# The opening of a two-layer adaLN kernel: raw weights in four homes over two queues, modulation in the filter's waits, the first normalisation between the spectra

## The reference, cut to what matters

```
h = layernorm(x) * (1 + ca) + sa ; x = x + ga * hyena(h)      # layer 0
h = layernorm(x) * (1 + cb) + sb ; x = x + gb * sign_ffn(h)
h = layernorm(x) * (1 + ca) + sa ; x = x + ga * attention(h)  # layer 1, 16 heads, causal
h = layernorm(x) * (1 + cb) + sb ; x = x + gb * experts(h)    # 2 of 8
gates: g = (2 * (g >= 0) - 1) * max(|g|, 0.25)
filter k = (sin-MLP of three layers on a position code) @ wo * decay
```

## Time and profile before

| | us |
|---|---|
| median of 3 runs (lowest, highest) | 1976.02 (1970.32, 1976.5) |
| the profiled execution | 1987.1 |
| its span | 1985.3 |
| first `up_rows` matmul in it | 115.12 |

### The profile page before, as it was taken

One profiled execution on the slowest core, in us unless ns is written; L12 is line 12 of the kernel. 1 busy time (PEld: TensorE's weight loads), 2 busy tenths in 40 slices (PEclk: granted clock), 3 DMA queues, 4 the chain that ended last, 5 costly groups with the idle time before them and its releaser, 6 DMA issues.

```text
span 1985.3 us, 27255 instructions
## 1 busy us (share of the span) xinstructions
PE 1790.3 (90%) x9220; PEld 1445.2 (73%) x9220; DVE 1455.8 (73%) x2643; ACT 997.5 (50%) x2142; POOL 684.9 (35%) x709
## 2 busy tenths in 40 slices
PE   6778879999988969999989979999999996999997
PEld 3657767777777857777877767777777785777786
DVE  4468877887468777887566887888746887888744
ACT  1132446777341437777632325677734143776742
POOL 0023244544123144553323234454412414455321
PEclk7879989999989979999989988999999997999999
DMA  6330054443060043443251024445225004354311
GB/s 241 110 129 1 9 157 112 98 123 76 28 259 1 1 127 102 124 109 80 50 217 54 0 57 125 107 99 132 60 71 211 1 1 127 102 131 125 77 28 48
DMA packets 90127, 184.14 MB, mean 93 GB/s; under 512 B 28991, under 2 KB 43135, under 8 KB 86790
## 3 DMA queue, kind: packets, MB, share of 16 engines
q1 hardware_dynamic: 82694, 168.77, 29.2%
q10 hardware_dynamic: 7296, 13.63, 2.4%
HBM read 125.46 MB, written 46.94 MB: 87 GB/s over the span
## 4 chain that ended last, share of the span: by engine, by line
PE 69%; DVE 12%; ACT 5%; issue 4%; DVEq 3%; POOL 3%; DMA 1%; ACTq 1%; SPq 1%; POOLq 0%; another core or an unknown queue 0%
PE ps L434 9%; PE ps L557 8%; PE ps L577 7%; PE ps L579 6%; PE ps L600 6%; PE ps L597 6%; PE ps L598 6%; PE ps L744 6%; PE ps L440 4%; PE ps L786 3%; PE ps L646 2%; PE ps L583 2%; PE ps L494 1%; PE ps L512 1%; ACT hT L823 1%
## 5 line engine op out<-in xcount | busy, mean ns | idle before, releaser
L1145 DVE CUSTOM_DVE_ANT_0 ps<-ps,mrow 128x128 f32<-128x128 f32 (+7 forms) x512 | 385.0, 765 | 118.2 <-PE ps L557 116.2
L1376 POOL TENSOR_TENSOR psplit<-pT,psplit 128x384 fp32r<-128x384 f32 (+3 forms) x320 | 302.3, 958 | 427.2 <-ACT psplit L866 425.1
L866 ACT ACTIVATE psplit<-ps 128x512 fp32r<-128x512 f32 (+3 forms) x768 | 373.2, 486 | 0.0
L865 ACT ACTIVATE pT<-ps 128x512 f32<-128x512 f32 (+3 forms) x512 | 256.7, 501 | 170.3 <-PE ps L583 91.0
L557 PE MATMUL ps<-khl,qhh 128*128 128x512 f32 (+3 forms) x768 | 252.9, 394 | 61.0 <-DMA qhh<-psplit 38.0
L577 PE MATMUL ps<-qhh,khl 128*128 128x512 f32 (+3 forms) x768 | 271.8, 354 | 7.6 <-ACT psplit L866 7.0
L579 PE MATMUL ps<-q,k 65*128 65x512 f32 (+3 forms) x768 | 268.5, 350 | 0.0
L597 PE MATMUL ps<-psplit,vhi 128*65 128x512 f32 (+3 forms) x768 | 264.8, 345 | 0.0
L600 PE MATMUL ps<-psplit,vhi 128*65 128x512 f32 (+3 forms) x768 | 259.8, 338 | 0.0
L598 PE MATMUL ps<-psplit,vlo 128*65 128x512 f32 (+3 forms) x768 | 259.3, 338 | 0.0
L557 PEld LDWEIGHTS ps<-khl,qhh 128*128 128x128 f32 x768 | 132.2, 202 | 80.1 <-issue 59.3
(11 more groups left out here) (188 smaller groups left out, 3402.8 us busy)
## 6 DMA issues: line engine op xcount, KB each, us to landing
qhh<-q_scratch SPq DMA_DIRECT2D x112, 256.0 KB, 5.1
q_scratch<-hrow SPq DMA_DIRECT2D x24, 1024.0 KB, 7.1
mix<-inverse_scratch SPq DMA_DIRECT2D x64, 256.0 KB, 3.5
q<-q_scratch SPq DMA_DIRECT2D x56, 256.0 KB, 4.6
Kf<-kf_scratch SPq DMA_DIRECT2D x3, 3072.0 KB, 20.5
khl<-k_scratch SPq DMA_DIRECT2D x24, 256.0 KB, 7.7
sgn<-sgn_scratch SPq DMA_DIRECT2D x6, 1024.0 KB, 14.1
x<-in_x SPq DMA_DIRECT2D x5, 1024.0 KB, 5.5
```

Of the source, the lines that this page charges most:

```text
L865: A(full(n)[:, 0:hi - lo], ps[:, b, 0:hi - lo], ACT.Exp, scale=SCALE)
L866: A(psplit[:, n % PRING, 0, 0:hi - lo], ps[:, b, 0:hi - lo], ACT.Exp, scale=SCALE)\
L1145: V.tensor_tensor_reduce(out=v, in0=v, in1=mrow[:, L - n:L], scale=1.0, scalar=-3e38, op0=ALU.add, op1=ALU.max, accum_out=mx[:, u % 2, i:i ...
L1376: G.tensor_tensor(psplit[:, n % PRING, 1, 0:m], full(n)[:, 0:m], psplit[:, n % PRING, 0, 0:m].bitcast(F32), ALU.subtract)\
```

## The change

- **Loads.** ScalarE issues five: cT, `wmod0`, `w2T`, `wmod1`, `in_w`. SyncE issues the rest. The four that filter layer 0 needs have a semaphore of their own; the other five have `loaded_layers`. `w1T`, the windows, `w1rows`, the two halves of `wqkv`, x and the (now 11) small ones have semaphores too.
- **Homes.** `wmod0` stays in `spare`, `wmod1` goes into `Kf` blocks 0 and 1, raw `in_w` into `Kf` block 3, the halves of `wqkv` into `wo` and `rope`, which are loaded after the split (`loaded_late`).
- **TensorE's order**: filter 0, three quarters of `modT` 0, filter 1, the last quarter, gate 0, `alpha2`, filter 2, `modT` 1, kernel rows, gate 1, spectrum 0, transposes of the first normalisation, spectra 1 to 3, then the batch. Setup banks are given by hand.
- **VectorE's order**: two angle steps, `modT` 0, third angle step, gate 0, `alpha1`, `modT` 1, kernel rows, gate 1, normalisation, split of `in_w`, `h_low`, mix 0, bounds of both gates, mix 1, split of `wqkv`, mix 2, split of `wr`, mix 3.
- **SyncE** asks for x as soon as the signs are taken, does not load it again for batch 0, and makes its stores after the `wqkv` split. The gate rows go after the three weight stores; VectorE waits for that store ahead of its spectrum products.
- **The meeting goes**, with the clearing. Counts run on from the setup: `at` adds `MADE`. One set of bank accounts serves both.

The core of the diff:

```diff
+SETUP = -1
+MADE = {"mod_picked": 1, "var_done": 2, "rstd_done": 2, "hrow_done": 8, "hT_done": 4, "h_lo_done": 4}
...
+            wmod = [wraw, Kf[:, 0:2, :, :].rearrange("p m k n -> p m (k n)")]
+            in_raw = Kf[:, 3, :, :].rearrange("p k n -> p (k n)").rearrange("p (q n) -> p q n", q=ND)
+            qkv_raw = [wo[:, :, :].rearrange("p q n -> p (q n)")[:, 0:QKV],
+                       rope[:, :, :].rearrange("p c n -> p (c n)")[:, 0:QKV]]
...
-        def part_ends(eng, name):
-
-            eng.drain().then_inc(bar, 1)
-            eng.wait_ge(go[name], 1)
-            eng.sem_clear(go[name])
...
# TensorE
+            filtered(0)
+            modulation(0, (0, 1, 2))
+            filtered(1)
+            modulation(0, (3,))
+            gate(0)
             pe.wait_ge(*at("const_made", 1))
             pe.wait_ge(*at("abs_done", 1))
-            b = bk.take(pe, ("alpha2",))
+            b = bk.take(pe, ("alpha2",), at=GATE_BANK[1])
             for q in range(NH1):
                 i = mm(ps[:, b, 0:D], ones[:, :], w2T[:, q, :], start=q == 0, stop=q == NH1 - 1)
             i.then_inc(ready[b], 1)
+            filtered(2)
+            modulation(1, (0, 1, 2, 3))
+            pe.wait_ge(*at("filter_sine", 3))
+            for t in range(0, NT, 2):
+                b = bk.take(pe, ("kern", t), until=at("kern_done", t // 2 + 1), at=(6, 7, 0, 1)[t // 2])
...
+            gate(1)
+            pe.wait_ge(*at("loaded_windows", 16 * 3))
+            pe.wait_ge(*at("kern_done", NT // 2))
+            kernel_spectrum(0)
...
             for h in range(NHALF):
                 normed(0, h)
-            part_ends(pe, "tensor")
+            for m in range(1, NB):
+                kernel_spectrum(m)
# ScalarE
+            load = nc.scalar.dma_start
+            load(cT[:, :, :, :], d["cT"], allow_slow_non_contiguous=True).then_inc(s["loaded_c"], 16)
+            load(wmod[0], d["wmod0"]).then_inc(s["loaded_mod0"], 16)
+            load(w2T[:, :, :], d["w2T"]).then_inc(s["loaded_w2"], 16)
+            load(wmod[1], d["wmod1"]).then_inc(s["loaded_mod1"], 16)
+            load(in_raw, d["in_w"]).then_inc(s["loaded_in"], 16)
...
+            sines(0)
+            act.wait_ge(*at("loaded_w2", 16))
             A(sgn2[:, :, :], w2T[:, :, :], ACT.Sign).then_inc(s["sgn_done"], 1)
             act.drain()
             A(w2T[:, :, :], w2T[:, :, :], ACT.Abs).then_inc(s["abs_done"], 1)
+            sines(1)
+            act.wait_ge(*at("loaded_w1", 16))
...
+            sines(2)
# VectorE
+            angles(0)
+            angles(1)
+            modulation(0)
+            angles(2)
+            copy_gate(0)
+            dve.wait_ge(*at("loaded_rows", 16))
+            V.reduce_sum(alpha1[:, :], w1rows[:, :, :], AX, apply_absolute_value=True)
+            modulation(1)
...
+            copy_gate(1)
...
             pick_first(0)
             dve.wait_ge(*at("x_loaded", 16))
             for h in range(NHALF):
                 stats(x, range(4 * h, 4 * h + 4))
                 normed(0, h, x)
+            dve.wait_ge(*at("loaded_in", 16))
+            split([in_w[:, a, :, :] for a in range(2)], in_raw, s["raw_used"])
             for h in range(NHALF):
                 h_low(0, h)
-            part_ends(dve, "vector")
+            mix_spectrum(0)
+            for layer in range(2):
+                bound_gate(layer)
+            mix_spectrum(1)
+            dve.wait_ge(*at("loaded_qkv", 16 * 2))
+            for q in range(ND):
+                split([wqkv[:, a, q, :] for a in range(2)], qkv_raw[q], s["qkv_split"])
+            mix_spectrum(2)
+            dve.wait_ge(*at("loaded", 16 * NLOADED))
+            split([wr[:, a, :, :] for a in range(2)], wr_raw[:, :, :])
+            mix_spectrum(3)
...
+                dve.wait_ge(*at("gate_stored", 16))
                 for i in range(NB):
                     multiply(0, i, Yf[i]).then_inc(s["y_dve"], 1)
# SyncE
+            sp.wait_ge(*at("qkv_split", 2))
+            for dst, src in ((wo[:, :, :], d["wo"]), (rope[:, :, :], d["rope"])):
+                dma(dst, src).then_inc(s["loaded_late"], 16)
+            sp.wait_ge(*at("raw_used", 1))
             for n in flat:
                 dma(scratch[n], flat[n].bitcast(F32)).then_inc(weights_stored, 16)
+            sp.wait_ge(*at("gate_rows", 2))
+            dma(gate_scratch, grow[:, :, :].rearrange("b l n -> b (l n)")).then_inc(s["gate_stored"], 16)
             sp.wait_ge(*at("kf_mixed", NB))
             dma(kf_scratch, Kf[:, :, :, :].rearrange("p m k n -> p (m k n)")).then_inc(weights_stored, 16)
             sp.wait_ge(*at("gate_stored", 16))
-
-            sp.wait_ge(bar, 4)
-            sp.sem_clear(range(nums[0], nums[-1] + 1))
```

More of the change, by code:

```diff
@@ L310, in adaln_hyena_binffn_gqa_moe @@
         freed = [sem(f"freed{i}") for i in range(8)]
[L311 to L315, removed]
+        now = {"batch": SETUP}
         def at(name, n):
-            return s[name], n + now["batch"] * EACH.get(name, 0)
+            if now["batch"] == SETUP:
+                return s[name], n
+            return s[name], n + MADE.get(name, 0) + now["batch"] * EACH.get(name, 0)
         def m_loaded(u):
@@ L441, in sign_mm, with modulation @@
                 return i
[L442 to L447, removed]
+            MOD_BANK, GATE_BANK = (2, 5), (3, 4)
+            KINDS = (0, 1, 3, 4)
+            def modulation(layer, some):
+                if some[0] == 0:
+                    pe.wait_ge(*at("silu_done", 1))
+                    pe.wait_ge(*at(f"loaded_mod{layer}", 16))
+                    bk.take(pe, ("modT", layer), at=MOD_BANK[layer])
+                b = bk.held(("modT", layer))
+                for n in some:
                     for dt in range(ND):
@@ L457, in modulation, with filtered @@
                         i = mm(ps[0:B, b, n * D:(n + 1) * D], cT[:, layer, q, :],
[L458 removed]
+                               wmod[layer][:, q, kind * D:(kind + 1) * D], start=q == 0, stop=q == ND - 1)
                 i.then_inc(ready[b], 1)
[L461 to L464 removed]
+            def filtered(layer):
+                pe.wait_ge(*at("loaded_layers", 16 * 5) if layer else at("loaded_filter", 16 * 4))
                 if layer:
@@ L467, in _ @@
                 for h in range(NHALF):
-                    b = bk.take(pe, ("filter", layer, h))
+                    b = bk.take(pe, ("filter", layer, h), at=h)
                     w = fw1[:, :] if layer == 0 else fw23[:, layer - 1, :]
@@ L807, in _, with copy_spectrum @@
             A(w2T[:, :, :], w2T[:, :, :], ACT.Abs).then_inc(s["abs_done"], 1)
-            for m in range(NB):
+            sines(1)
+            act.wait_ge(*at("loaded_w1", 16))
+            A(sgn1[:, :, :], x[:, :, :].rearrange("p t n -> p (t n)").rearrange("p (q n) -> p q n", q=ND), ACT.Sign)\
+                .then_inc(s["sgn_done"], 1)
+            sines(2)
+            b = bk.wait(act, ("alpha2",))
+            A(alpha2[:, :], ps[:, b, 0:D], ACT.Copy, scale=1.0 / HID).then_inc(freed[b], 1)
+            def copy_spectrum(m):
                 b = bk.wait(act, ("kf", m, 0))
                 A(Kf[:, m, 2, :], ps[:, b, :], ACT.Copy).then_inc(s["kf_copied"], 1)
-            b = bk.wait(act, ("alpha2",))
-            A(alpha2[:, :], ps[:, b, 0:D], ACT.Copy, scale=1.0 / HID).then_inc(freed[b], 1)
             def normed(k, h, mod):
@@ L828, in _ @@
                 normed(0, h, modn)
-            part_ends(act, "scalar")
-            bk = banks["batch"]
+            for m in range(1, NB):
+                copy_spectrum(m)
             def high(k):
@@ L1005, in modulation, with angles @@
                 dve.drain()
-            dve.wait_ge(*at("loaded_filter", 16 * 9))
-            for layer in range(3):
+            def angles(layer):
+                dve.wait_ge(*at("loaded_layers", 16 * 5) if layer else at("loaded_filter", 16 * 4))
                 if layer:
@@ L1084, in pick_first @@
                               .rearrange("p n b -> p (n b)")).then_inc(s["mod_picked"], 1)
-            dve.wait_ge(*at("loaded_raw", 16 * 3))
-            split([in_w[:, a, :, :] for a in range(2)], wraw[:, :, 0:INNER], s["raw_used"])
-            split([wr[:, a, :, :] for a in range(2)], wr_raw[:, :, :])
-            dve.wait_ge(*at("loaded_raw", 16 * 4))
-            split([wqkv[:, a, :, :] for a in range(2)], wraw[:, :, :])
-            dve.drain()
             pick_first(0)
```

138 lines of the change are left out of this document (55 added, 83 removed).

## The result

The changed kernel takes 1955.5 us, the median of 4 runs (1951.9 to 1957.0), against 1975.6 (1970.3 to 1976.5) for the kernel before on the same chip: a ratio of 0.9889 with a 95% interval of 0.9867 to 0.9911. It is faster, by 20 us instead of the 34 forecast, and lies 0.5 us above the upper end of the range (as a ratio it is 0.9889, where 1955 against the 1976.0 of the forecast is 0.9894). Its profiled execution took 1954.8 us.

A forecast was written before the change was run, and what follows sets the result against it. The opening was taken as bound by low-clock TensorE work, then a VectorE and DMA tail. Moving the first up matmul from 115.1 to 83.2 us, plus 2.0, gave 33.9 off 1976.0: 1942 us, range 1933 to 1955.

The forecast's parts named there:

- Step 1: Opening: fourth filter load issued near 2.5 us and landed near 5.2, first filter layer done at 8.9.
- Rival C: Opening: two load queues share bandwidth and TensorE's order bites, up to 10.5 us more, 1946 to 1954; chance 0.24.
- Step 2: Opening: wmod0 issued near 1.8 us, landed at 9.0; three quarters of modT take 5.2, to 14.3.
- Steps 3 and 4: Opening: second filter layer, last modT quarter and gate to 24.7 us; alpha2 at 5.3, half low clock, half high, to 30.0.
- Step 5: Opening: third filter layer to 31.9 us, angles and sine to 38.7, second modulation (7.0) fitting beneath, to 39.0.
- Step 6: Opening: kernel matmuls 7.1 us at the low clock, gate 3.5, spectra starting at 49.8, 7.7 us earlier than before.
- Rival B: Opening: alpha2 lifts the clock and it stays, 6.9 us more gain, 1933 to 1939; chance 0.13.
- The middle: Spectra and first normalisation: hrow at 59.8 us, 96 spectrum records 20.9 plus 2.0 slow start, first up matmul at 83.2.
- VectorE beneath it: VectorE after hrow: 23.4 us of work, last mix about 84.6, needed at 89 at the earliest, slack 4 us.
- The cover: Moved SyncE stores cost nothing: gate rows stored near 97 us, gates loaded near 105, needed at 113 and 107.
- rival D: Gate rows queue behind SyncE's stores and VectorE waits: slower than 1976, chance 0.02; partly, 1954 to 1970, chance 0.04.
- The sum: Whole kernel: 31.9 us earlier first up matmul plus 2.0 behind it, 33.9 off the 1976.0 median, giving 1942.

The follow-up runs named there:

- filter_first: Changed kernel with ScalarE's wmod0 and the four loads behind it issued only once filter layer 0's four loads have landed: 1952.1 us, ratio 0.9859 to the kernel before.
- one_queue: Changed kernel with all opening loads on SyncE's one queue, the filter's four first, none issued by ScalarE: 1951.9 us, ratio 0.9835 to the kernel before.
- meeting: Changed kernel with the meeting of four engines put back ahead of the first batch, without clearing or SyncE: 1955.6 us, ratio 0.987 to the kernel before.
- a_again1: The changed kernel, unedited, in a second execution: 1951.7 us (one run), beside 1979.6 for the kernel before.
- alpha_late: Changed kernel with alpha2 moved behind the two matmuls of filter layer 2: 1953.5 us, ratio 0.985 to the kernel before.
- a_again2: The changed kernel, unedited, timed again against the kernel before on the same chip: 1954.4 us, ratio 0.9851.
- the repeat of before: The kernel before, unedited, in a second execution: 1981.2 us.
- alpha_fill: Changed kernel with alpha2 moved behind the second modulation, right ahead of the kernel matmuls: 1953.8 us, ratio 0.9847 to the kernel before.
- the second repeat of before: The kernel before, unedited, in a third execution: 1979.7 us.

## Why the prediction came out as it did, step by step

- **Step 1, the filter's loads: wrong.** "The fourth is issued near 2.5 and lands near 5.2 (0.3 us allowed for the other queue's packets)." Issued at 2.10, used at 10.68: with the other queue's loads under way it took 6.3 us more (8.54 less the 2.28 of filter_first), not 0.3, and the stage ended 5.5 us late. filter_first (2.28 us from issue to landing) and one_queue (TensorE at 4.46) show the cause. Rival C had priced the two queues but put their cost on `wmod0`, which took 7.1 us where it had taken 7.0, and on the layer weights; it is the four first loads that pay. The allowance had no row behind it. Nor does the large load's length bound it: `wmod0` landed 7.1 us after its issue at 1.16, and the four small ones were used 2.4 us after that. The second queue brought nothing in return: one_queue has the first `up` matmul at 81.79, where the two queues have it at 86.15.
- **Step 2, `wmod0` and three quarters of `modT`: right** (issued 1.16; 5.21 us against 5.2), only not what ended last.
- **Steps 3 and 4:** the order forecast held, each stage 5.3 to 5.6 us late. alpha2 took 3.65 instead of 5.3, which paid 1.7 back: to 33.64 against 30.0. It did not lift the clock itself. It ran at the high level from its first matmul on, where gate 0 had run at the low one (3.27, and 3.51 in the first repeat, ahead of the same 3.65). No run shows the 7.0 that step 4 has for alpha2 wholly at the low level: it took 3.65 to 5.67 us in the eleven traces of the changed kernel and its edits. The factor of two stands in other matmuls, 7.19 and 3.65 us for the kernel's. Half and half was a fair price, and the 1.7 were luck: in meeting, with the same code up to there, it took 4.86. Sine 2 was ready at 31.75, so 1.8 us were given away, not 3.7.
- **Step 5: right in its sum, by another way.** `modulation(1)` took 3.74 at the high level and then TensorE idled for 3.21. The sine, not modulation, ended the wait: 42.37 against 39.1.
- **Step 6: right.** Kernel matmuls 7.19 (7.1), gate 3.52 (3.5), both at the low level. The spectra start at 52.99 against 49.8. Rival B had the clock rise with alpha2, which came true, and stay, which did not. The forecast was right to expect the low level here, but the clock did not need an idle gap to fall. The first window below shows the gap, with nothing on TensorE, and the next the stretch behind it; in a_again1 the clock fell before the gap, under the narrow matmuls of `modulation(1)`. In six of the eight traces with this order it fell so, while TensorE was busy, and in two in the gap; in alpha_late it fell without any gap. What lowers it is not isolated:

```profile
39.20:42.30 3.10, 0.00 (x0) 0.00 (x0) 2.98 (x4) 1.04 (x2) 0.00 (x0) 0.61 0.96 306
42.30:49.50 7.20, 7.13 (x17) 5.12 (x18) 4.22 (x8) 0.28 (x2) 1.29 (x7) 0.50 0.01 4
64.00:67.00 3.00, 3.00 (x9) 2.45 (x8) 2.82 (x3) 0.69 (x2) 0.00 (x0) 0.50 0.00 0
```

- **The middle: right.** From the first statistics to the last `hrow` 9.1 us (9.15). After the transposes the spectra start at the low level again (0.50 in the last of these windows), and the 96 records took 22.20 (22.9 forecast). Of the 5.5 us from step 1, 2.95 are left at the first `up` matmul: 86.15 against 83.2.
- **VectorE beneath it, and the first batch: right.** The last mix ended at 87.82, 3.2 us later than forecast like all else, and the tap came 4.04 us after the first `up`: 2.0 gained. Down to the last output store the three traces of before took 1864.9 us in the mean and those of the changed kernel 1860.2, so 4.6 less where 2.0 were priced; of the other 2.6 no run shows the place.
- **The cover: right, rival D false.** SyncE waited 12.1 us for the gate rows' store, and went on at 100.26 (97 was forecast); the load of `gates` landed 8.9 us later, at 109.2 (105). GpSimd's first sum with gates waited 0.87:

```profile
109.19 0.73 POOL L1452 TENSOR_TENSOR mix<-rows,mix 128x256 f32<-128x256 f32 x1 [0.87 <-DMA mix<-gate_scratch]
```

  Its counterpart of the 7.89 us idle ahead of 154.61 is 6.78 us at 123.60, so the 0.87 was hidden.
- **The sum: its base was wrong.** "Nothing shows where those 11 us lie ... so it comes off the median whole." The gain was worked out against an execution whose opening was 6.0 us slower than in two other traces of the same kernel, by the clock of the kernel matmuls and the spectra, while the time it came off was a median. 33.9 less 6.0 for the base and 2.95 for the stages is 25.0, and with the 2.6 behind the first `up` matmul it is 27.6. The medians give 20.1 (this measurement), 30.1 (a_again2) and 27.9 (the single run of a_again1). So the 6.0 and the 2.95 are shown in traces, and they account for the two later comparisons within 2.5 us. They do not account for this one: the other 7.5 us of it are open. All four runs of before lie at 1970.3 to 1976.5 here, and all 21 on the three later occasions at 1978.1 to 1987.8, while the changed kernel's hardly differ (1951.9 to 1957.0, later 1951.7 to 1956.2). That the two profiled executions differ by 32.3, so near to 33.9, is partly luck: 2.95 less than forecast in the opening stand against 1.3 more behind it (3.3 for 2.0), and the slow base is in both figures.
- **The rivals.** 1955.5 lies just above rival C's 1946 to 1954, but of C only a cost of the two queues came true, at another place; alpha2 was quick and VectorE was not late. Of the signs listed, the first `up` matmul (86.15, for 80 to 86), alpha2's end (33.6, for 28 to 32), the spectra's start (53.0, for 48 to 52), the last DMA on the chain (10.6, for 10) and the gate store (100.2, for 100) were just missed, with the delay of step 1 ahead of all of them; the others held.

**Open.** The median of the kernel before was 1975.6, 1979.6, 1984.5 and 1980.3 on four occasions, that of the changed one 1955.5 and 1954.4 on two, with 1951.7 once. I have no trace of an execution of the kernel before near 1975, so I can't say what is quick in it; the chip is not ruled out, since the three later occasions were on three chips. By what the large loads hold the small ones up, and which of them does it, was not told apart either: filter_first holds back all four of them. That they share the DMA engines, as rival C and the text of filter_first have it, no run isolates.

## What to carry to other kernels

Small loads that start the program should not be under way together with large ones on another queue: hold the large back until they land, or put them behind in one queue, and do not price the large ones at a few tenths: here they cost the small ones 6.3 us while the first large one took no longer (7.1 us, and 6.9 with the small ones ahead of it). Where an execution's stretch shows the clock at its low level behind idle time, look at a second trace of the same kernel before the gain there is taken off a median. A filler put into an idle gap paid here because the clock was high again behind it (the kernel matmuls took 3.65 us instead of 7.19), but price the fillers themselves at the low level (`modulation(1)` took 6.71 us and alpha2 5.67, instead of 3.74 and 3.65). Judge a change of a few us by landmarks stage by stage, not by a total alone; and take two traces for that too, since the same opening put this landmark 6.0 us apart in two traces of one kernel.

## What the runs showed of the hardware

- Four small loads (0.2 to 12 KB) on SyncE's queue were used 8.3 to 8.8 us after the last's issue (10.35 to 10.94 in the eight executions with the two queues as the change has them) with 4.75 MB issued on ScalarE's queue at 1.2 to 3.6 us, and 2.3 us after it with those held back. The first 1.5 MB load (`wmod0`) took 6.7 to 7.1 us either way.
- Being busy did not raise the clock in every stretch: in the repeat of before TensorE was busy for 13.77 of 14.00 us with narrow matmuls (4 columns or 64 rows) at 0.50, and in alpha_fill for 6.60 of 6.60 at 0.52; after alpha2's dense 128x256 matmuls it was at 1.00 (5.40 of 5.40 us busy). Nor did it need idle time to fall: in alpha_late it went from 1.00 to 0.50 within the kernel matmuls, with TensorE busy for over 13 us ahead of that. So TensorE's busy share alone does not tell which level a stretch gets.
- The same code took either level in the same place in different executions: 7.12, 3.65 and 4.08 us for the kernel matmuls of before, 3.74 and 5.86 for `modulation(1)` of the changed kernel.
- The granted clock that a trace records can read 1.00 where matmuls run at the low level, ahead of its first recorded fall: 3.64 us for the second filter layer at 21.28 in the changed kernel, and 6.92 us for 32 modulation records in the second repeat of before, over 35 to 49 us. A duration next to it tells.
